# GpSimd splits the keys of the last two batches after the first residual adds of the down projection

## What is computed

```python
x = x + jnp.tanh(g_xattn[0]) * _L0_xattn_ref(ctx_1024, _layernorm(x, axis=-1))       # time-warping alignment
x = x + jnp.tanh(g_ffn[0]) * _L0_ffn_ref(_layernorm(x, axis=-1), w1, conv_w, conv_b, w2)
x = x + jnp.tanh(g_xattn[1]) * _L1_xattn_ref(_layernorm(x, axis=-1), ctx_1024, ctx_1024, ...)
x = x + jnp.tanh(g_ffn[1]) * _L1_ffn_ref(_layernorm(x, axis=-1), ...)                # top-k memory network

# _L0_ffn_ref
h = bit_linear(x, w1)                 # 256 -> 1024
h = silu(depthwise_conv1d(h, conv_w, conv_b))
return bit_linear(h, w2)              # 1024 -> 256
# bit_linear: every token's row is scaled to 127/max|row|, rounded, multiplied by ternary weights, scaled back

# _L1_xattn_ref: 16 heads of 16, 375 keys per batch
k = (key @ Wk.T + bk)
out = softmax(q * HEAD_DIM ** -0.5 @ k.T) @ v
```

## Time and profile before

| | us |
|---|---|
| median of 3 runs | 606.16 |
| lowest, highest of the 3 | 601.97, 606.25 |
| the profiled execution, device time | 607.65 |
| its span | 605.7 |
| TensorE busy (72%) | 436.5 |
| VectorE busy (70%) | 423.3 |
| ScalarE busy (45%) | 274.3 |
| GpSimd busy (13%) | 80.9 |

### The profile page before, as it was taken

How to read it: one execution, slowest core, us unless ns; L and a number is a source line. 1 busy time by engine, 2 the same in 40 slices (tenths; PEclk the granted TensorE clock), 3 DMA queues, 4 the chain that set the end, 5 groups by cost and what they waited for, 6 DMA issues and landing times.

```text
span 605.7 us, 10407 instructions
## 1 busy us (share of the span) xinstructions
PE 436.5 (72%) x3507; PEld 302.3 (50%) x3507; DVE 423.3 (70%) x1719; ACT 274.3 (45%) x657; POOL 80.9 (13%) x233
## 2 busy tenths in 40 slices
PE   3799799723275996757999999999999664702106
PEld 3468586611154654634777777676455464201103
DVE  7545999899947678957788888875454666276673
ACT  3744544723223543434365566665533553254440
POOL 6790000000050445421000000000000000000000
PEclk9998699855568898668599999999999987855556
DMA  9700003297004975400054948900300272000002
GB/s 275 205 1 2 1 2 127 78 171 149 11 25 122 136 145 139 120 9 1 2 73 70 209 74 141 208 2 1 139 2 1 77 270 71 0 1 1 1 1 61
DMA packets 34666, 47.23 MB, mean 78 GB/s; under 512 B 5542, under 2 KB 32055, under 8 KB 32823
## 3 DMA queue, kind: packets, MB, share of 16 engines
q1 hardware_dynamic: 34614, 46.58, 32.9%
HBM read 37.87 MB, written 8.60 MB: 77 GB/s over the span
## 4 chain that ended last, share of the span: by engine, by line
PE 58%; DVE 22%; ACT 11%; issue 5%; POOL 4%; DVEq 0%; POOLq 0%; ACTq 0%
PE ps L2175 8%; PE ps L2129 4%; PE ps L2105 4%; DVE PR L1049 4%; PE ps L2116 4%; ACT below L1769 4%; PE ps L1910 4%; PE ps L2022 3%; PE ps L1918 3%; PE ps L2091 3%; PE ps L2301 3%; PE ps L1974 2%; DVE prod L1045 2%; DVE below L1395 2%; PE ps L1869 2%
## 5 line engine op out<-in xcount | busy, mean ns | idle before, releaser
L1263 DVE TENSOR_REDUCE negm<-ps 112x1 f32<-112x375 f32 x128 | 66.2, 544 | 12.6 <-PE ps L2105 9.7
L1740 ACT ACTIVATE E<-ps 125x448 f32<-125x448 f32 x96 | 52.2, 544 | 43.6 <-PE ps L2116 43.4
L2274 PE MATMUL ps<-cnt,same 128*128 128x3 bf16 (+4 forms) x40 | 7.0, 174 | 61.5 <-ACT below L1769 41.1
L2105 PE MATMUL ps<-ks,qs 96*112 96x375 bf16 x128 | 46.3, 375 | 3.0 <-ACT qs L1733 2.0
L2129 PE MATMUL ps<-E,v 125*32 125x112 f32 x768 | 42.2, 270 | 0.2 <-issue 0.2
L2116 PE MATMUL ps<-qs,ks 99*125 99x112 bf16 x384 | 40.1, 228 | 0.5 <-ACT E L1740 0.5
L1251 DVE TENSOR_REDUCE acts<-gel 128x4 f32<-128x448 f32 x32 | 19.8, 621 | 29.3 <-ACT gel L1708 29.3
L2116 PEld LDWEIGHTS ps<-qs,ks 99*125 99x125 bf16 x384 | 34.9, 141 | 9.1 <-issue 6.2
L2274 PEld LDWEIGHTS ps<-cnt,same 128*128 128x128 bf16 (+1 forms) x40 | 4.5, 113 | 65.2 <-issue 65.2
L1708 ACT ACTIVATE gel<-ps 128x448 f32<-128x448 f32 x32 | 17.3, 544 | 29.3 <-PE ps L2175 29.3
L789 POOL CAST kp<-kx 128x750 bf16<-128x750 f32 x8 | 6.9, 862 | 166.0 <-ACT path L1623 126.1
(11 more groups left out here) (384 smaller groups left out, 1115.1 us busy)
## 6 DMA issues: line engine op xcount, KB each, us to landing
ks<-key_parts SPq DMA_DIRECT2D x48, 187.5 KB, 6.7
piw<-fn_process_input_weights SPq DMA_DIRECT2D x8, 1024.0 KB, 4.8
key_parts<-kp SPq DMA_DIRECT2D x48, 93.8 KB
ctx_again<-in_ctx SPq DMA_DIRECT2D x7, 512.0 KB
keys<-kx SPq DMA_DIRECT2D x16, 187.5 KB, 2.2
kx<-keys SPq DMA_DIRECT2D x8, 375.0 KB, 6.8
ctxP<-in_ctx SPq DMA_DIRECT2D x8, 256.0 KB, 6.5
patn<-in_L_ffn_input_patterns SPq DMA_DIRECT2D x1, 2048.0 KB, 17.2
```

The source lines that it names most:

```text
L1263: drain(dve.tensor_reduce(negm[:, n:n + 1], bank(nm)[0:S, 0:SC], AX.X, ALU.max, negate=True), nm)
L1740: drain(fn(E[:, (KCH * f + c) % 6, :], bank(nm)[0:KC, 0:4 * S], ACT.Exp), nm)
L2105: fill(mm(bank(nm)[0:S, 0:SC], qs[0:SR, u // 4 % 3, n, :], ks[0:SR, u // 4 % 3, n, :], start=True, stop=True), nm)
```

## The change

GpSimd gets one wait more. Ahead of the split of batch 6, it waits until `x_ready` is 10, that is, until VectorE has added the down projection's result to batches 0 and 1. Batches 6 and 7 are then split, and what follows on GpSimd stands behind them as before. No instruction that computes or moves data is added or taken away.

```diff
             wait_drained(pool, ("ffn_up", 0, 1))
             for b in range(2, B):
+                if b == B - 2:
+                    pool.wait_ge(x_ready, B + 2)
                 split_keys(b)
             wait_drained(pool, "bo")
             pool.wait_ge(ln_ready, 3 * B)
```

## The result

The changed kernel took 600.09 us in the median of 11 runs (597.56 to 603.79); the kernel before, run beside it, 602.56 in the median of 11 (601.11 to 606.25). The ratio over all these runs is 0.9943, with a 95% interval of 0.9919 to 0.9968 (the two medians alone would give 0.9959). Two later timings of the same pair gave 0.9944 (0.9915 to 0.9972) and 0.9956 (0.9924 to 0.9989). So the change saves 0.4% to 0.6%, some 2.7 to 3.4 us (the medians differ by 2.1 to 3.6): well under 1%, and yet clear of no change in each of the three.

The account below looks back on a forecast made before the run. The prediction saw a chain mostly through TensorE and VectorE, with VectorE instructions held by GpSimd splits. Token rows 3.5 plus roundings 0.76 less `nmr` 1.3 gave 3.0 us, from 606.16 to 603.2; range 599.5 to 606.8.

Parts of the forecast that it names:

- Steps 1 to 3: Ahead of the down projection: scales ready 2.78 us earlier, second token rows ending 3.5 earlier, roundings 0.76 shorter together.
- `nmr` is not held: At the first `nmr` behind the residual adds: no wait for GpSimd, so 4.3 us saved, 601.9; chance 0.20.
- a rival at up to 3.05: First half's query product: the clock comes back sooner, up to 3.05 us more saved, 600.1; chance 0.10.
- its own sign of being wrong: The forecast would be wrong if, among others, the query products' 6.30 and 3.25 us changed.
- step 4: Down projection on TensorE: 0.28 us of idle covers the difference between the earlier start and the last rounding; nothing lost.
- Slack and queues: Behind `nmr`: about 5 us cover lengthened normalisations, bias adds meet only the first half's split, delayed SyncE loads are covered.
- Nothing happens: What VectorE saves is waited for elsewhere, above all in the down projection at half clock: 606.2; chance 0.08.
- clock later: Query products: the low clock reaches over the second product and first query stacks, 4.55 us lost against 3.0, 607.8; chance 0.12.

Follow-up runs that it names:

- a1_after: The changed kernel timed and profiled again with no edit; ratio to the kernel before 0.9956 (0.9924 to 0.9989).
- e1_after_nmr: Changed kernel, but the splits of batches 6 and 7 wait until behind the first half's `nmr`; ratio to the kernel before 0.9960 (0.9928 to 0.9992).
- e2_one_add: Changed kernel, but GpSimd waits for one residual add less (`x_ready` at 9), so its splits start earlier; one run, 599.79 us.
- e7_bias_late: Changed kernel, but splits 6 and 7 wait behind the first `nmr` and the bias adds behind the last query split; ratio to before 0.9899 (0.9852 to 0.9947).
- e4_stores_only: Kernel before with its splits in place; only SyncE's stores of batches 6 and 7 wait for the second residual add; ratio 0.9985 (0.9956 to 1.0015).

## Why the prediction was right or wrong

**The mechanism and the stretch: right.** Steps 1 to 3 stand in the profile as they were worked out: the scales at 0.17, the second token rows at 1.36 (near 1.3 expected; the clock fell 0.6 us before their end), roundings at 0.62. The first residual add came 4.21 us earlier against the joining reduction, 4.3 was the sum. `nmr` took 1.33, 1.4 was expected, and ended with line 795. The Trainium skill's rule on this ("SBUF — State Buffer", section "Who interferes with whom": two SBUF inputs contend, and who came first has the ports for the whole instruction) agrees with `nmr` at 1.33 and, started 0.39 later against GpSimd, at 0.94. The prediction called `asc` in agreement too; it has one SBUF input only, so it bears on how long the hold lasts, not on this rule's condition. `nmr` in these two profiles closes what the trace of before had left open, and the rival "`nmr` is not held" falls.

**What the sum left out: 0.4 us.** 3.0 expected, 3.40 measured up to the first score maximum. ScalarE's normalisation came 3.05 earlier, as summed up; the rest is the first query product, 5.95 for 6.30, in which the clock came back 3.8 us sooner than before while the product began only 3.0 sooner. The prediction had this as a rival at up to 3.05 and took it at nothing; by its own sign of being wrong (the 6.30 changed) this term of the sum was mis-sized, by 0.35. It is no fixed number: 5.88 and 6.15 in the two other profiles of the same kernel.

**The down projection (step 4): right, without anything to spare.** I had 0.28 us of TensorE's idle time covering a difference of 0.25. The 64 matmuls now run as one piece of 9.55 with no idle time, so from its start on TensorE sets the time there, and of the roundings only the first still counts. In a1_after the first eight ran at the upper level, took 1.08, and TensorE then waited 0.54 for ScalarE; the first residual add came no later for it (14.34).

The step also needed something that the prediction did not work out: that the clock comes back as much earlier as the product starts. It did. One microsecond of the kernel before and one of the changed kernel, with the rise in each:

```profile
253.00:254.00 1.00, 1.00 (x10) 1.00 (x9) 1.00 (x2) 0.40 (x1) 0.00 (x0) 0.94 0.00 0
```

```profile
248.00:249.00 1.00, 1.00 (x8) 1.00 (x8) 1.00 (x2) 0.59 (x2) 0.00 (x0) 0.70 0.00 0
```

The rise came at 253.1 and at 248.6, 13.7 and 10.0 behind the joining reduction, 4.3 and 4.5 behind the start of the product (3.7 to 5.4 in the thirteen profiles here). Had it stayed at 13.7, another 3.7 us of the product would have run at half the clock, and some 1.8 of the gain would have been lost (an estimate from these rows). That the sum holds here is in part luck.

**Slack and queues: right.** VectorE's two normalisations lasted 1.97 for 0.73 and ended 5 us ahead of their use; the second half's query split has 0.63 an instruction. The experiment with the bias adds alone confirms that the bias adds had cover. But the cover was not as wide as it read: with `nmr` out of the way the same bias adds fell on the second half's split and took back the gain (e1_after_nmr). The longest wait of SyncE's queue for scores went from 53.7 to 38.4:

```profile
SPq L611 <- PE ps L2118: 87.3, 5, 38.4
```

**The absolute time: wrong by its base.** I set 3.0 us against a median of three runs, 606.16. With eleven runs the median of the same kernel is 602.56. The changed kernel, at 600.09, lies near the lower end of the range for that reason, not because the saving was larger than thought. In ratios the prediction is 603.2 to 606.16, 0.9951, inside each of the three measured intervals. Three runs of which two agree within 0.1 us looked like a firm base with one low outlier; the lone 601.97 was the usual case and the other two are the highest of the eleven.

**The chances: the step that failed.** I took 1%, 6 us, as what a measurement of this kernel can tell from no change, and from that gave 0.90 to "no difference". The ground was the 4.3 us over which three single runs spread; single runs of the changed kernel spread over 5 to 8, but eleven of each kernel told 0.57% with an interval of 0.25% to either side, and two further timings told 0.56% and 0.44%. The time did stay within 1%, and it is a gain all the same. A sum of 3 us that rests on measured rows, with the rivals that cancel it at 0.2 together, should have been called one, if a small one. "Nothing happens" and "clock later" did not occur in any of the three profiles of the changed kernel.

**Left open.** The clock's part. Low for 10.2 us around the first query product in the changed kernel (from 20.2 to 30.4 behind the joining reduction), in e2_one_add and in the kernel before, 6.8 in e1_after_nmr, e7_bias_late and e4_stores_only. In these profiles TensorE's transposes began 1.2 to 2.4 us after the fall, and the length does not follow from that alone: 1.7 before and 1.5 in e4_stores_only, with 10.2 and 6.8. Nor does it follow from the program: in a1_after, the changed kernel again, the clock fell 3 us sooner, 5.4 ahead of the transposes, and was low for 13.7. No run here takes the clock apart from the order of the work, so whether the 1.1 us of e7_bias_late come with its order or could be lost again in another execution is not settled; they came in both profiles of it. Nor is it settled why the search loses them again.

## What to carry to other kernels

An instruction that is many times longer than its tile asks for, on an engine that the profile calls busy, is probably a wait: set its end beside the ends of the instructions on the other engines. When work on that other engine is moved, walk its new place instruction by instruction and ask of each neighbour whether it can be held; a tiny one on the chain pays the rest of a long one, here 1.2 us for four numbers a partition, and what stands behind the moved work in the queue moves as well and can hit the next stage. Judge an edit of a few microseconds by a stretch from an event that it cannot move to one behind it, in two profiles of either kernel; then look whether the rest of the program keeps what the stretch has won, and take the base from more than three runs.

## What the runs showed of the hardware

- VectorE's instruction is held for the rest of one GpSimd instruction, not for its whole run, and a tile of 112x4 then ends about 0.02 us behind it: `nmr` at 1.33, 0.94, 0.85 beside half an instruction, and 0.16 when it came at the end of one. A rounding of 128x896 ends 0.48 behind it (in the kernel before at 248.80, the cast beside it at 248.32). With both engines issuing back to back they take turns, one instruction each: 0.98 us for each bias add in e1_after_nmr (7.87 for eight), 0.75 in the changed kernel.
- Held were: scales of 112x4 with one SBUF input, roundings of 128x896, casts, and instructions with two SBUF inputs. Not held: reductions (0.69 and 0.17), reciprocals (0.18), batch statistics (0.41 to 0.42), and additions of a PSUM and an SBUF tile (0.45 to 0.47), all of them beside splits in the changed kernel or the one before.
- The spread of the whole time goes with TensorE's mean granted clock. In the first eleven runs of the changed kernel the four with a mean of 0.834 took 597.56 to 599.12 us, the four with 0.826 took 600.09 to 601.22, the one with 0.821 took 603.79. It goes with it only roughly: the two with 0.829 and 0.828 took 599.76 and 601.77. The program is the same in all.
